# Adaptive-norm attention block: values alone between score pairs, other matmuls regrouped, means subtracted at use, no unread lead products

## The reference, cut to what matters

```python
x = L0_attn_x                                    # (16, 256, 128), float32
mod = (_silu(L0_c) @ L0_wmod).reshape(16, 6, 1, 128)
sa, ca, ga, sb, cb, gb = (mod[:, i] for i in range(6))
ga, gb = sign(ga) * max(|ga|, .25), sign(gb) * max(|gb|, .25)
h = _layernorm(x) * (1 + ca) + sa
x = x + ga * attention(h)      # 16 heads of 8, softmax(q k^T) / sqrt(128), W_out, b_out
h = _layernorm(x) * (1 + cb) + sb
x = x + gb * ffn(h)            # h and weight rounded to a 6-bit grid in blocks of 32, h @ w.T + bias
```

## Time and profile before

| | |
|---|---|
| runs shown | 272.79, 273.89, 275.31 us, median 273.89 |
| profiled execution | 273.2 us, of which the span from first to last instruction is 271.4 us |
| PE busy | 252.9 us, 93% of the span |
| DVE busy | 233.0 us, 86% |
| ACT, POOL busy | 205.9 us (76%), 185.3 us (68%) |
| chain that ended last | 78% on PE, 9% on DVE, 3% on DMA |
| mean granted TensorE clock | 0.991 |

### The profile page before, as it was taken

The page is one execution under the profiler, slowest core; times in us unless marked ns, Lnnn a source line. Parts: engine busy times, 40 slices in busy tenths (PEclk is TensorE's granted clock), DMA queues, the critical chain, the costliest instruction groups (busy, mean ns, idle before and its releaser), DMA issues.

```text
span 271.4 us, 7574 instructions
## 1 busy us (share of the span) xinstructions
PE 252.9 (93%) x2568; PEld 165.2 (61%) x2568; DVE 233.0 (86%) x597; ACT 205.9 (76%) x414; POOL 185.3 (68%) x384
## 2 busy tenths in 40 slices
PE   2679999999999999999999999999999999999952
PEld 2356666666676666666666666666667666565631
DVE  6579997999899999999999999999998889852264
ACT  5255787978797879797979888887978777777620
POOL 5814071869777878787878888797978655637550
PEclk9999999999999999999999999999999999999996
DMA  5465577364726555364637362627263630100000
GB/s 140 119 184 156 148 231 194 108 172 141 191 86 174 163 138 161 101 208 129 185 96 193 117 182 93 196 98 195 93 180 109 179 116 24 45 24 22 0 31 31
DMA packets 21654, 34.94 MB, mean 129 GB/s; under 512 B 3408, under 2 KB 17504, under 8 KB 19696
## 3 DMA queue, kind: packets, MB, share of 16 engines
q1 hardware_dynamic: 18688, 31.71, 40.1%
q10 hardware_dynamic: 2928, 2.75, 3.3%
HBM read 22.88 MB, written 9.99 MB: 121 GB/s over the span
## 4 chain that ended last, share of the span: by engine, by line
PE 78%; DVE 9%; issue 3%; DMA 3%; SPq 2%; ACTq 2%; POOL 1%; ACT 1%; POOLq 0%; DVEq 0%
PE ps_p L1026 26%; PE ps_o L1056 21%; PE ps_pre L1078 5%; PE ps_p L1041 5%; PE ps_post L1109 3%; DVE neg_max L837 3%; PE ps_o L1095 3%; PE ps_post L1123 3%; PE ps_pre L1085 2%; PE ps_p L1156 2%; PE ps_pre L1072 2%; PE ps_post L1117 2%; PE ps_pre L1065 2%; DMA q_rows<-maxT 1%; ACTq L393 1%
## 5 line engine op out<-in xcount | busy, mean ns | idle before, releaser
L837 DVE TENSOR_REDUCE neg_max<-ps_p 128x2 f32<-128x512 f32 x256 | 164.1, 681 | 10.5 <-PE ps_p L1026 9.0
L653 ACT ACTIVATE probs<-ps_p 128x512 f32<-128x512 f32 x256 | 139.3, 596 | 20.6 <-PE ps_p L1041 16.4
L1026 PE MATMUL ps_p<-k_rows,q_rows 62*128 62x256 f32 x512 | 97.9, 307 | 0.7 <-DVE neg_max L837 0.4
L1041 PE MATMUL ps_p<-q_rows,k_rows 64*128 64x256 f32 x512 | 98.1, 308 | 0.4 <-DMA q_rows<-maxT 0.4
L1026 PEld LDWEIGHTS ps_p<-k_rows,q_rows 62*128 62x128 f32 x512 | 69.2, 185 | 29.8 <-DVE neg_max L837 12.9
L1041 PEld LDWEIGHTS ps_p<-q_rows,k_rows 64*128 64x128 f32 x512 | 69.7, 185 | 4.7 <-ACT probs L653 2.3
L1056 PE MATMUL ps_o<-probs,v_aug 128*32 128x256 f32 x1024 | 68.5, 385 | 0.3 <-ACT probs L653 0.3
L1056 PEld LDWEIGHTS ps_o<-probs,v_aug 128*32 128x32 f32 x1024 | 26.7, 109 | 20.0 <-ACT probs L653 0.8
L499 POOL CAST max_parts<-neg_max 128x16 fp32r<-128x16 f32 x32 | 6.3, 197 | 40.1 <-DVE neg_max L837 40.1
L525 POOL TENSOR_TENSOR qk_parts<-qk_full_sb,qk_parts 128x256 fp32r<-128x256 f32 x28 | 20.4, 730 | 2.3
L1078 PE MATMUL ps_pre<-hT,wqk_sb 128*128 128x256 f32 x56 | 17.9, 402 | 1.8 <-ACT hT L623 1.0
(11 more groups left out here) (142 smaller groups left out, 360.1 us busy)
## 6 DMA issues: line engine op xcount, KB each, us to landing
q_rows<-q_dram SPq DMA_DIRECT2D x30, 256.0 KB
k_rows<-k_dram SPq DMA_DIRECT2D x60, 128.0 KB
modb<-mod_rows_dram SPq DMA_DIRECT2D x16, 256.0 KB, 3.7
q_dram<-qk_parts SPq DMA_DIRECT2D x28, 128.0 KB, 2.4
k_dram<-qk_parts SPq DMA_DIRECT2D x28, 128.0 KB, 2.4
out_dram<-out_sb SPq DMA_DIRECT2D x16, 128.0 KB, 1.8
x_all<-in_L_attn_x_dram ACTq DMA_DIRECT2D x6, 256.0 KB, 4.4
q_rows<-maxT SPq DMA_DIRECT2D x64, 8.0 KB
```

The costliest lines, as they stand in the source:

```text
L653: act.activation(probs[:, v % 2, u % 4, :], ps_p2[:, (16 * b + u) % P2_BANKS, :], ACT.Exp).then_inc(exp_done, 1)
L837: dve.tensor_reduce(neg_max[:, half, :, r, j], ps_p1[:, (16 * b + s) % P1_BANKS, :].rearrange("p (q k) -> p q k", q=QT), AX_X, ALU.max, ne ...
L1026: ins = pe.matmul(ps_p1[:, (16 * b + s) % P1_BANKS, t * T:(t + 1) * T], q_rows[64 * r:64 * r + ROWS1, slot, i, t * P:(t + 1) * P], k_rows[ ...
L1041: ins = pe.matmul(ps_p2[:, (16 * b + u) % P2_BANKS, t * T:(t + 1) * T], k_rows[64 * r:64 * r + ROWS2, slot, i, t * P:(t + 1) * P], q_rows[ ...
```

## The change

The step structure stays. What moves or goes:

- PE: behind a quarter of `values` no other work follows before the next pair. `transpose_max(b+1, 0)` goes from s = 6 to s = 8, next to `project_v` and `project_out`; `transpose_hd(b-2)` from 12 to 14; `transpose_x` from s = 0 of its step to s = 14 of the step before; both `project_qk` run at s = 4, with `transpose_norm`; `linear` goes from s = 14 of step b to s = 2 of step b+1, behind `transpose_o`. The last blocks keep some old places.
- PSUM: the bank `ps_pre` is used in both halves (`ps_pre`, `ps_pre_b`), with extra waits so that ACT reads no half while PE writes the other.
- ACT: the copies follow their producers (`hdT` at s = 0, `hT` at 2, q and k at 5 and 7, `onT` at 6, first `maxT` at 9, v at 10).
- DVE: `finish(b-3)` goes from s = 0 to s = 4. L752 is gone everywhere: the users of the mean subtract it themselves, in the same number of operations. `stats1(3)`, `aggregate1(3)` come earlier in the setup.
- POOL: `quantise` stands ahead of `ffn_weights`. One memset of the setup is gone.
- SP: `store(b-3)` stands ahead of `place_max(b+1, 0)`.
- Lead phase: no `unread_lead`; the product for k of block 2 goes from s = 12 to s = 14 of step -2.

The core of the diff:

```diff
-                dve.tensor_tensor(nm[:, :], mv[:, :, 0], minus_one[:, :], ALU.mult)
                 return dve.tensor_tensor(ve[:, :], mv[:, :, 1], eps[:, :], ALU.add)
...
-                    elif s == 0 and has(b - 3) and b - 3 != LAST - 1:
+                    elif s == (0 if b - 3 == LAST - 2 else 4) and has(b - 3) and b - 3 < LAST - 1:
                         finish(b - 3)
...
-                    ffn_weights(b - 2)
                     quantise(pool, b - 2)
+                    ffn_weights(b - 2)
                     residual2(b - 2)
...
-                    if b < 0 and has1(b, s):
-                        unread_lead()
...
-                    if s == 0 and pre:
-                        transpose_x(c, (maxT_saved, 2 * (b + 1)), (v_saved, 1))
...
-                    if s == 2 and pre:
-                        project_qk(c, 0, q_full, ps_pre[:, :])
+                    if s == 2 and has(b - 3) and b - 3 < LAST - 2:
+                        linear(b - 3)
                     if s == 4 and pre:
-                        project_qk(c, 1, k_full, ps_pre[:, :], (q_saved, c - FIRST + 1))
+                        project_qk(c, 0, q_full, ps_pre[:, :], (maxT_saved, 2 * (b + 1)))
+                        project_qk(c, 1, k_full, ps_pre_b)
...
+                    if s == 14 and in_steps(c + 1) and c + 1 > FIRST:
+                        transpose_x(c + 1, ps_pre_b, (v_saved, b + 2), (maxT_saved, 2 * (b + 1) + 1))
```

More of the change, by code:

```diff
@@ L459, in _ @@
                     load_modb(b + 1)
+                if has(b - 3):
+                    store(b - 3)
                 if has(b + 1):
                     place_max(b + 1, 0)
-                if has(b - 3):
-                    store(b - 3)
                 if in_steps(c):
@@ L618, in _, with save_hT @@
             act.wait_ge(modT_ready, 1)
-            def save_hT(c):
-                wait(act, (xT_full, c + 1), (v_full, c - 2))
-                act.activation(hT[:, c % 3, :], ps_pre[:, :], ACT.Identity, scale=scaleT[:, c:c + 1],
+            def save_hT(c, src=ps_pre, *before):
+                wait(act, (xT_full, c + 1), (v_full, c - 2), *before)
+                act.activation(hT[:, c % 3, :], src, ACT.Identity, scale=scaleT[:, c:c + 1],
                                bias=shiftT[:, c:c + 1]).then_inc(hT_saved, 1)
@@ L641, in save_v, with save_maxT @@
                                ).then_inc(v_saved, 1)
-            def save_maxT(b, half):
-                wait(act, (maxT_full, 2 * b + half + 1), (max_placed[half], 32 * b))
+            def save_maxT(b, half, *before):
+                wait(act, (maxT_full, 2 * b + half + 1), (max_placed[half], 32 * b), *before)
                 act.activation(maxT[:, half, :], ps_pre[0:16, 0:T], ACT.Copy).then_inc(maxT_saved, 1)
@@ L693, in _ @@
                         exponentials(b, s)
+                    if s == 0 and has(b - 3) and b - 3 < LAST - 2:
+                        save(b - 3, hdT_full, f_full, hdT[:, :], ps_post[:, :], hdT_saved)
                     if s == 1 and b - 1 == LAST:
@@ L721, in _ @@
                         load_x(act, b + 6)
-                    if s == 9 and has(b + 1) and b >= 0:
-                        save_v(b + 1)
+                    if s == 10 and has(b + 1) and b >= 0:
+                        save_v(b + 1, ps_pre_b)
                     if s == 13 and b - 2 == LAST:
@@ L727, in _ @@
                                       (f_full, LAST))
-                    elif s == 13 and has(b - 2) and b - 2 != LAST - 1:
+                    elif s == 13 and b - 2 == LAST - 2:
                         save(b - 2, hdT_full, f_full, hdT[:, :], ps_post[:, :], hdT_saved)
@@ L814, in _ @@
             dve.tensor_tensor(wblk(wf_d), wblk(wf_q), spread(wf_sc), ALU.mult).then_inc(wfd_ready, 1)
+            stats1(FIRST + 1)
+            aggregate1(FIRST + 1)
             dve.wait_ge(rows_copied, 1)
@@ L827, in _ @@
             first_low_part(1, 1)
-            stats1(FIRST + 1)
-            aggregate1(FIRST + 1)
             def maxima(b, s):
@@ L1152, in linear_last @@
                           ).then_inc(last_f_full, 1)
-            def unread_lead():
-                pe.matmul(ps_p2[:, 0, 0:T], wqk_sb[:, 0, :], hT[:, 1, :], start=True, stop=True)
             def unread(b):
@@ L1229, in _ @@
                         values(b, 0)
-                    if s == 6 and has(b + 1):
+                    if s == (6 if b == -1 else 8) and has(b + 1):
                         transpose_max(b + 1, 0, (k_saved, c - FIRST + 1) if in_steps(c) else (maxT_saved, 2 * (b + 1)))
+                    if s == 8 and has(b + 1) and b >= 0:
+                        project_v(b + 1, ps_pre_b)
                     if s == 8 and b - 1 == LAST:
@@ L1237, in _ @@
                         project_out(b - 1)
-                    if s == 8 and has(b + 1) and b >= 0:
-                        project_v(b + 1, ps_pre, (maxT_saved, 2 * (b + 1) + 1))
                     if s == 10 and has(b):
@@ L1246, in _ @@
                             transpose_hd_last(t)
-                    elif s == 12 and has(b - 2) and b - 2 != LAST - 1:
+                    elif s == (12 if b - 2 == LAST - 2 else 14) and has(b - 2) and b - 2 < LAST - 1:
                         transpose_hd(b - 2)
+                    if s == 14 and in_steps(c + 1) and c + 1 > FIRST:
+                        transpose_x(c + 1, ps_pre_b, (v_saved, b + 2), (maxT_saved, 2 * (b + 1) + 1))
                     if s == 14 and has(b + 1):
@@ L1253, in _ @@
                             linear_last(t)
-                    elif s == 14 and has(b - 2) and b - 2 != LAST - 1:
+                    elif s == 14 and b - 2 == LAST - 2:
                         linear(b - 2)
```

73 lines of the change are left out of this document (36 added, 37 removed).

## The result

The changed kernel takes **294.52 us** (median of 4 runs, 293.91 to 295.03) beside 274.38 us for the kernel before (4 runs, 272.79 to 275.31). The ratio is 1.074, with a 95% interval of 1.068 to 1.080: slower, by some 20 us. The profiled execution took 295.03, with a span of 291.9 us; the span before was 271.4, so 20.5 us are to be found.

A forecast was written before the change was run, and what follows sets the result against it. PE's list (14.30 us a block) bound the kernel; POOL's loop through DVE (14.33) would bind next. Ten steps +1.4, lead -2.0, first blocks -0.6, last -1.2: -2.4 us, profiled 273.2 to 270.8, median 271.5, range 266 to 277.5.

The forecast's parts named there:

- the part on the means: DVE's L752 goes and users subtract the mean at no cost; L752 and L753 together valued at 0.16 us per block of DVE.
- the 144.3 forecast: Ten steps from the scales of step 2 to those of step 12: 144.3 us against 142.95, a term of +1.4.
- the 1.0 that the sum had on top of ten times 14.33: Ten steps: less 0.5 for the first x1b, plus 1.2 for later copies and DMAs, plus 0.3 for late head 8.
- The loop: Scales, `finish` at s = 4, x1b, x_res, split of maxima, h2, scales, through DVE and POOL: from 12.80 to 14.33 us.
- The clock in the lead phase: Rival, chance 0.10: without unread products PE's clock falls, block 0 starts at half clock, +1.5 us, time 273.0.
- forecast -2.0 for the lead: Lead phase without unread products: DVE sets the pace, first second scores about 2 us earlier; -2.0 us, bounds 0 and -2.6.
- Later copies and DMAs: Path of the maxima rows through SP, 12.8 to 14.4 us, mostly under 14.33; 1.2 us over ten blocks, bounds 0 and 6.6.
- L753 meets x_res: Rival, chance 0.20: L753 of `stats2` on DVE falls into POOL's x_res every block; period about 15.1, time 277.4.
- PE's regrouping: `transpose_hd`, `transpose_x` and first `transpose_max` join runs: 0.41 us less per steady block, PE's bound from 14.30 to about 13.9.

The follow-up runs named there:

- The exchange of one word: Changed kernel with `add` in place of `subtract` in POOL's two normalising lines, operands unchanged (so the mean is added): 285.23 us, ratio 1.040.
- the kernel with early maxima: Changed kernel, first-half maxima transposed at s = 6, copied at s = 7, k copied at s = 5: 291.40 us with `subtract`; 278.17 adding a negated mean from one DVE operation.
- the kernel with late maxima: Changed kernel with POOL's two normalising lines using `add` for `subtract`, first-half maxima still copied at s = 9: 285.23 us, ratio 1.040.
- the fastest kernel: Changed kernel with early maxima, negated mean and variance from one DVE operation, `finish` at s = 3, lead products back, two more unread products in block 0: 272.36 us, 0.993.

## Why the prediction was wrong

It said 271.5 us, with a range to 277.5 and a chance of 0.21 for slower; it is 294.5.

**The step that failed** is in the part on the means: "Subtracting at use costs nothing, being the same number of operations." The number of operations is the same and POOL's four take 0.35 us more each, 1.39 a block. The trace before has no call on POOL of that form with `subtract`, so no row gave a price; it was set to nothing, with no room above, and no rival stood for it. Ten blocks of 1.39 on the loop are 13.9 us, and the ten steps took 158.3 for the 144.3 forecast. (That the two differences are so near is in part chance: the fall of the clock in block 10 added 0.7 and ten handoffs 0.3, and the 1.0 that the sum had on top of ten times 14.33 did not show.) The exchange of one word shows the cause (9.3 us in the changed kernel), short calls in the kernel with early maxima give 13.2, and the kernel before shows what the calls with `subtract` cost where the loop has slack: 1 us.

**The loop** was right, and was the term that decides. The prediction followed it piece by piece to 14.33 us; with short calls and nothing in the way it is 14.46, and with the dearer ones 15.75 = 14.33 + 1.39 and 0.03. `amax` waits for h, x1b for `finish`, POOL has no idle time ahead of the second split, all as written. What was not drawn from it: a loop that has become the bound turns each further delay on it into time, so the other edits on it had to be priced with more care than before.

**The clock in the lead phase** had a chance of 0.10 and a price of +1.5. It came, and the kernel before without the products lost 2.8 us by it, though the lead got 1.1 shorter. The price was low because block 0 was taken as 3 us of PE work at half clock with a part covered; block 0 took 3.4 us more. The row that spoke against it, PE at 2 to 7 tenths in the first slices at full clock, is for the most part of the time in which the lead's pairs were not yet running. The longest gap ahead of the fall was 0.3 us. The Trainium skill (TensorE: Matmul & The Clock Gate, A second HAM failure mode: psum-queue depth-cycling) tells of a kernel whose clock went up and down by frequent short idle times between groups of matmuls. The trace agrees in part: short gaps, five of 0.1 us in the last 3.30, came ahead of the fall; but the clock fell once and stayed at half for 17 us, and the kernel before kept the full clock behind 2.27 us busy in 3.00. What exactly brings it down stays open; that leaving out the lead's products does is shown by the kernel before: its mean clock went from 0.99 to 0.95 or 0.96 without them, in all four runs. Of the forecast -2.0 for the lead the trace has -0.7; its last 7 us ran at half clock, and no run shows the lead without the products at full clock.

**Block 0** by itself was not looked at. The regrouping leaves its first slots light, and in the trace with the lead's products back it still takes 3.2 us more than before (15.58 for 12.40).

**Later copies and DMAs** were priced at 1.2 us over the ten blocks, from a path of 12.8 to 14.4. The path was right, its length not: 15.7 in the crowded block shown, since the sum had no term for the issue ahead of the last landing (0.68) and the landing took 4.33. It costs 1.7 to 3.1 us in the changed kernel, mostly in block 1 (15.31 for 14.13). With POOL's short calls the kernel with late maxima takes 7 us more (285.23 for 278.17), in which a second fall of the clock, in block 1, has its part.

**L753 meets x_res** did not happen, since the dearer calls move x_res away. It happens to L752 where that is kept, and gives 15.13, the period that the prediction worked out for L753. With short calls and no L752 (285.23 us) L753 begins 0.02 to 0.03 ahead of x_res in five of nine steady blocks and takes 0.16, and once 0.27 behind it and takes 0.47; so the margin was thinner still than the 0.1 to 0.3 of the prediction.

**PE's regrouping**: forecast 0.41 a block (0.30 with the first `transpose_max` where it was); 0.1 is the most that any kernel here shows. `transpose_hd` and `transpose_x` no longer cost what they did in s = 12 and s = 0 (these pairs of pairs go from 2.15 and 2.12 us to 1.75 and 1.76). But `linear` in the place of q at s = 2 makes that slot 0.13 longer, where q's 0.66 against some 0.5 for `linear` promised 0.1 less or more, and the run of three at s = 14 costs 0.7 and not 0.56. Which part of this is PE's own and which is DVE's and POOL's pace there (PE's loads wait 0.8 us a block for DVE's maxima in the fastest kernel) was not tried.

## What to carry to other kernels

The same count of instructions is no price: when an operation code changes on an engine, time one call of it, or give it a bound of its own as if it were new. Ask of each edit which loop it lies on after all the other edits are in, for what is hidden in the old order can be the bound in the new. And look at the granted clock of each stretch in which taking work away, or regrouping it, leaves TensorE with short idle times: the first block of a pipeline has only part of the steady list.

## What the runs showed of the hardware

- GpSimd's `tensor_scalar` on 128x128 fp32 takes 0.80 us with `subtract` then `mult`, and 0.45 with `add` then `mult`, with the same operands. VectorE's `scalar_tensor_tensor` of the same shape takes 0.35 us either way.
- TensorE's granted clock fell to half with no gap over 0.32 us in the 7 us ahead (changed kernel, 2.81 us busy in the last 3.30), and in the kernels without the lead's products stayed there for 17 to 20 us, through stretches in which TensorE counted as busy throughout (3.70 of 3.70). In the kernel before it stayed full behind 2.27 us busy in 3.00.
- A VectorE operation with two inputs in SBUF that began 0.03 us behind a GpSimd operation of 0.74 took 0.72 in place of 0.16, and moved a whole period by 0.7. One that began 0.03 us ahead of it took 0.16.
